# A two-layer attention and mixture-of-experts kernel: the first router's logits made with tokens on the partitions, and GpSimd's scatters of a batch issued in one go

## What is computed

```python
logits = jax.nn.relu(x @ rw1 + rb1) @ rw2 + rb2      # rw1 128x512, rw2 512x8
vals, ids = jax.lax.top_k(logits, K)                 # K = 2 of E = 8
probs = jax.nn.softmax(vals, axis=-1)
...
m = jax.nn.one_hot(ids_f, E, dtype=jnp.int32)
pos = jnp.cumsum(m, axis=0) - 1                      # place in the expert's queue
...
disp = jnp.zeros((E, CAP, Cx), x.dtype).at[ids_f, pos_c].add(xr * keep[:, None])
h = jax.nn.relu(jnp.einsum('enc,ech->enh', disp, ew1) + eb1[:, None, :])
eo = jnp.einsum('enh,ehc->enc', h, ew2) + eb2[:, None, :]
y = eo[ids_f, pos_c] * (probs_f * keep)[:, None]
```

## Time and profile before

| | |
|---|---|
| median of 3 runs | 906.22 us (905.99 to 906.40) |
| the profiled execution | 906.78 us, of which the span from the first to the last instruction is 905.0 us |
| granted TensorE clock over the span | 0.966 |
| PE busy | 772.4 us (85%) |
| DVE busy | 684.2 us (76%) |
| ACT busy | 629.4 us (70%) |
| POOL busy | 630.8 us (70%) |

### The profile page before, as it was taken

One profiled execution on the slowest core, in us unless ns is written; L12 is line 12 of the kernel. 1 busy time (PEld: TensorE's weight loads), 2 busy tenths in 40 slices (PEclk: granted clock), 3 DMA queues, 4 the chain that ended last, 5 costly groups with the idle time before them and its releaser, 6 DMA issues. The chain is left out here.

```text
span 905.0 us, 18379 instructions
## 1 busy us (share of the span) xinstructions
PE 772.4 (85%) x6152; PEld 468.8 (52%) x6152; DVE 684.2 (76%) x2029; ACT 629.4 (70%) x972; POOL 630.8 (70%) x416
## 2 busy tenths in 40 slices
PE   3978656678998799288889989999999999999997
PEld 1344212224443366132235757777777777777775
DVE  7859999975775587598999878666767666666654
ACT  3755333414445587168889988898989888889895
POOL 5008999810677546466998997686868686868695
PEclk9979898999999799689999999999999999999999
DMA  5899400018100120442600000000000000000000
GB/s 152 118 119 185 147 0 0 18 27 236 33 16 7 44 63 25 126 112 56 196 1 1 1 3 1 13 0 12 0 12 0 12 0 12 0 0 12 0 14 13
DMA packets 52794, 40.48 MB, mean 45 GB/s; under 512 B 6060, under 2 KB 44735, under 8 KB 52735
## 3 DMA queue, kind: packets, MB, share of 16 engines
q1 hardware_dynamic: 49662, 37.28, 18.7%
q0 software_dynamic: 3072, 2.51, 1.0%
HBM read 18.07 MB, written 14.88 MB: 36 GB/s over the span
## 5 line engine op out<-in xcount | busy, mean ns | idle before, releaser
L759 POOL TENSOR_TENSOR scratch<-scratch 128x1024 f16<-128x1024 f32 x128 | 272.8, 2134 | 84.6 <-ACT scratch L1216 82.4
L1877 DVE SCALAR_TENSOR_TENSOR resid<-PS,coef,resid 128x128 f32<-128x128 f32 x512 | 144.0, 344 | 108.7 <-PE PS L1929 103.2
L1929 PEld LDWEIGHTS PS<-A,scratch 128*128 128x128 f16 x3456 | 203.4, 98 | 37.8 <-POOL scratch L759 4.8
L1929 PE MATMUL PS<-A,scratch 128*128 128x128 f16 x3456 | 217.1, 219 | 3.9 <-POOL scratch L759 1.6
L1929 PE MATMUL PS<-A 128*128 (+1 forms) x768 | 186.8, 379 | 0.7 <-issue 0.2
L1212 ACT ACTIVATE scratch<-PS,cols 128x512 f32<-128x512 f32 x256 | 163.8, 683 | 25.8 <-PE PS L1929 18.9
L1216 ACT ACTIVATE scratch<-scratch 128x1024 f16<-128x1024 f32 x128 | 135.3, 1057 | 5.0
L1929 PE MATMUL PS<-scratch,ident 128*128 128x512 f32 x160 | 85.0, 651 | 41.1 <-DVE scratch L1392 41.0
L624 POOL TENSOR_TENSOR scratch<-A 128x1024 f32<-128x1024 f32 x32 | 75.7, 2393 | 59.1 <-DVE A L1363 56.7
L1929 PEld LDWEIGHTS PS<-A 128*128 128x128 f16 x768 | 70.7, 98 | 66.5 <-issue 0.7
L669 POOL DMA_INDIRECT disp<-A,scratch x64 | 62.9, 982 | 36.5 <-issue 30.1
(11 more groups left out here) (342 smaller groups left out, 1332.9 us busy)
## 6 DMA issues: line engine op xcount, KB each, us to landing
A<-A SPq DMA_DIRECT2D x22, 256.0 KB, 7.5
y_rows<-zeros SPq DMA_DIRECT2D x8, 512.0 KB, 6.0
A<-y_rows SPq DMA_DIRECT2D x14, 256.0 KB, 3.9
disp<-zeros SPq DMA_DIRECT2D x4, 528.0 KB, 21.3
resid<-in_L_attn_x SPq DMA_DIRECT2D x8, 256.0 KB, 3.8
A<-scratch SPq DMA_DIRECT2D x8, 256.0 KB, 7.2
A<-in_L_ffn_ew SPq DMA_DIRECT2D x1, 2048.0 KB, 12.7
A<-scratch SPq DMA_DIRECT2D x32, 64.0 KB, 2.0
```

The lines of the kernel that those rows point to most:

```text
L759: pool.tensor_tensor(h_low[n % 4], h_full[n % 2], h_high[n % 4], SUB).then_inc(S("m1_low"), 1)
L1877: last = STT(out=resid[:, g, :], in0=bank(4 + e % 2)[:, t * C:(t + 1) * C], scalar=coef[b % 2][:, t, e:e + 1], in1=resid[:, g, :], op0=MUL ...
L1929: return nc.tensor.matmul(o, l, r, start=start, stop=stop)
```

## The change

`router_logits_T` and the transposes go, and so does ScalarE's copy. `router_logits(b)` now holds a 128x128 tile of the hidden layer and streams the 128x8 weights: 4 tiles of tokens by 4 parts of the hidden layer, 16 f32 matmuls of 8 columns, straight into bank 5 with tokens on the partitions. It stands where `router_logits_T` stood, ahead of `transpose5(b+1)`. It waits for VectorE to have read the last batch's logits out of bank 5. `relu5` waits for `lg5_mm` instead of `lgT5_mm`. GpSimd's wait ahead of the fifth scatter goes. ScalarE waits for its own last `hid5` before it uses banks 0 to 3 for the weights.

```diff
                 for t in range(NT):
-                    if t == NT // 2 and b + 1 < B:
-                        pool.wait_ge(S("lg5_mm"), at(b + 1))
-                    elif t == NT // 2:
-                        pool.wait_ge(s_eb2_mm, 1)
                     for k in range(TOP0):
...
-                act.wait_ge(S("lgT5_mm"), at(b, 2))
+                act.wait_ge(S("lg5_mm"), at(b, 2))
...
-            def lgT5_copy(b):
-                act.wait_ge(S("lgT5_mm"), at(b))
-                act.wait_ge(S("lg5_mm"), at(b, 1))
-                A_(lg5_T, bank(5)[0:E0, :], ACT.Copy).then_inc(S("lg5_T"), 1)
...
-                lgT5_copy(b)
...
+            act.wait_ge(S("hid5"), at(B * HC0 - 1))
             for k in range(EARLY):
...
-                TT(lg5[u], bank(6)[:, 0:NT * E0].rearrange("p (n e) -> p n e", e=E0),
+                TT(lg5[u], bank(5)[:, 0:NT * E0].rearrange("p (n e) -> p n e", e=E0),
...
-            def router_logits_T(b):
+            def router_logits(b):
                 pe.wait_ge(S("hid5"), at(b * HC0 + HC0 - 1))
-                pe.wait_ge(S("lg5_T"), at(b, 1))
-                for h in range(HC0):
-                    last_mm = mm(bank(5)[0:E0, :], w_r2[:, h, :], hid[b % 2][:, h, :], start=h == 0, stop=h == HC0 - 1)
-                last_mm.then_inc(S("lgT5_mm"), 1)
-
-            def router_logits(b):
-                pe.wait_ge(S("lg5_T"), at(b))
-                pe.wait_ge(S("placed"), at(b, 1))
-                for t in range(NT):
-                    last_mm = nc.tensor.transpose(bank(6)[:, t * E0:(t + 1) * E0], tile(lg5_T, t), ident[0:E0, 0:E0])
+                pe.wait_ge(S("lg5_added"), at(b, 1))
+                for t in range(NT):
+                    for h in range(HC0):
+                        last_mm = mm(bank(5)[:, t * E0:(t + 1) * E0], tile(hid[b % 2][:, h, :], t), w_r2[:, h, :],
+                                     start=h == 0, stop=h == HC0 - 1)
                 last_mm.then_inc(S("lg5_mm"), 1)
...
-                router_logits_T(b)
+                router_logits(b)
                 if b + 1 < B:
                     transpose5(b + 1)
                 if b and b + 2 < B:
                     variance_o(b + 2)
-                router_logits(b)
                 if b == 0:
```

More of the change, by code:

```diff
@@ L128, in build @@
                     "r0_decay", "r_coef", "p2_copied", "o_sq", "o_std", "x_std",  "hid5",
-                    "rows5", "lg5_T", "m0_hid",  "m1_cT", "m1_hid", "m1_high",
+                    "rows5", "m0_hid",  "m1_cT", "m1_hid", "m1_high",
                     "xn7",  "kq_high", "v_copied7", "gk_copied", "sg_7", "gate_ln", "gate_high",
@@ L136, in build @@
                     "gate_low", "yg1_ready", "z_added",   "mlp_added", "xn12", "split_low", "m0_low", "xdT", "x_low", "lg12_added", "lg_less", "z_stats", "hid11_low"],
-            "pe": ["transposed", "proj_q", "proj_k", "proj_b", "proj_g", "proj_v", "ss_head", "r0_acc", "r_q", "r_acc", "p2_mm", "centred", "o_var", "proj_o",  "hid5_mm", "lgT5_mm", "lg5_mm", "counts", "trd",
+            "pe": ["transposed", "proj_q", "proj_k", "proj_b", "proj_g", "proj_v", "ss_head", "r0_acc", "r_q", "r_acc", "p2_mm", "centred", "o_var", "proj_o",  "hid5_mm", "lg5_mm", "counts", "trd",
                    "m0_hid_mm", "m0_out_mm", "m1_cT_mm", "m1_hid_mm", "m1_out_mm", "m1_bias_mm",  "kq_mm", "v_mm7", "g_mm7", "gk_mm", "r1_k", "r1_e",
@@ L380, in build @@
         id5 = [v.rearrange("p (k n) -> p k n", k=TOP0) for v in routing(192, 8)]
-        lg5_T = carve(8)[0:E0, 512:1024]
         place = by_expert(carve(8)[:, 0:32])
```

## The result

The changed kernel took **920.19 us** (median of 4 runs, 919.71 to 923.03), the kernel before 906.31 beside it (4 runs, 905.99 to 907.47): a ratio of 1.015, 95% interval 1.0138 to 1.0162. The forecast was 904.6 with a range up to 909.6. It became slower, by the way that the prediction held for the first of its rivals: TensorE's clock falls behind the new logits.

The account below looks back on a forecast made before the run. GpSimd's scatters were taken to decide stage 5's end, by 0.7 us over the barrier. Batch 0's 1.1 plus GpSimd's 0.55 gave 1.65 us: 906.22 - 1.65 = 904.6 us, own range 903.9 to 905.2, whole range 903.5 to 909.6.

Parts of the forecast that it names:

- the first of its rivals: Stage 5: TensorE's clock falls in the new logits and the kernel gets slower, 926 us (915 to 945); 16 in 100.
- TensorE's clock: Stage 5: 4.8 us of few columns per batch might lower the clock; the forecast took it as staying at 1.00.
- Against it: TensorE is never idle there: Argument against the clock falling in stage 5's new logits, a case given 16 in 100.
- So little streaming makes it fall: Stage 5: read from the clock's fall to 0.50 at 298, behind 4 us with twelve small matmuls.
- 3 more: Steady batches, if the clock falls and is back halfway: a batch costs 3 us more, 20 us over seven batches.
- The new logits: TensorE, stage 5: 32 instructions at 0.105 us each, 3.4 us, hidden in steady batches behind the wait for `normalise5`.
- Batch 0: Stage 5's first batch: routing starts 1.1 us earlier, and this gain is carried to batch 6.
- the 0.55: GpSimd, batch 6: without the middle wait its scatters start 0.55 us (0.44 to 0.66) sooner after their slots.
- the contention of scatters and VectorE might fall too: Stage 5: aside in the rival that GpSimd's whole 3.94 us wait comes back, 902.9 or better; 8 in 100.
- What is late next: End of stage 5: SP and stage 6 follow the scatters; the barrier strand, its slots 2.2 us earlier, stays in front.
- the barrier strand: Entry of stage 6: TensorE passes the barrier and runs unread matmuls, done 0.7 us before the scatters let stage 6 start.
- the rival of 0.125 an instruction: Stage 5: `transpose5` waits for slower new logits, 0.3 us in each of five batches, 906.6 us; 7 in 100.

Follow-up runs that it names:

- the run of the scatters alone: The kernel before with only GpSimd's wait in the middle of a batch's scatters left out: 907.44 us, ratio 1.0015.
- few columns: The kernel before with 14 unread f32 products of 128x8 added behind the old logits of each batch: 944.30 us, ratio 1.042.
- many columns: The kernel before with 15 unread f16 products of 128x512 added behind the old logits of each batch: 930.37 us, ratio 1.0266.

## Why the prediction was wrong

**The step that failed** is the choice in "TensorE's clock": "Whether loading keeps the clock up no row tells", and the sum then went by a clock of 1.00 with 16 in 100 on the other side. The runs show that it does not stay up in this stretch. Behind 28 or 32 loads of 128x128 with 8 columns each, it is at 0.50 in every batch, though the engine is busy; behind the same time with 512 columns a load it is not. "Against it: TensorE is never idle there" was the wrong argument. It is true, 69.9 of 70.0 us, and has no weight. "So little streaming makes it fall" turned out right, but its row did not show it: in the 4 us ahead of 298 TensorE was busy for only 0.76, so idleness would have explained that fall as well. All seven falls in the trace of the kernel before come behind 4 us in which TensorE was busy for 2.5 us or less.

**The size of that rival** was 20 us (926); it is 14. The pieces held: a fall lengthens the work from `variance_o` to the next logits by 8.80 - 5.91 = 2.9 us in the batch at 269.9, as its "3 more". But the step between routings grows by 1.94 us on the mean. In some batches the clock is back sooner: the step from 246.4 grew by only 1.6. And the loop is no longer the one through VectorE: before, TensorE idled 8.8 of 71 us, and this slack takes the first part of the longer work.

**The new logits** are 32 instructions in 231.60 - 227.92 = 3.68 us, 0.115 each, where 0.105 was taken and 0.101 to 0.125 were the bounds. At 1.00 they would still be hidden behind the 3.78 until `normalise5`, but with 0.1 to spare, not 0.3.

**Batch 0** won 0.4 and not 1.1. From the start of the logits to the routing it is 218.88 - 215.10 = 3.78, against 4.73 before: 0.95 of the 1.1 is there. But the logits start 0.55 later (215.10 for 214.55): stage 5 began 0.35 later, a difference from stages that the change does not touch, and the six matmuls ahead of the logits took 1.66 for 1.46. Nothing was carried on: the clock is down from 218.8.

**GpSimd.** That each batch starts 0.8 after its slots was right: 240.60 against slots at 239.8 (in batch 0 it is 0.96, 225.52 against 224.56). So was the 0.55, with 0.44 to 0.66 around it: in the run of the scatters alone batch 6 starts at 291.48, 0.78 after its slots and not 1.44. What was missed is that the place of the scatters against VectorE's work changes too. That "the contention of scatters and VectorE might fall too" was named, with the wrong sign: 1.3 us later in that run.

**What is late next.** The prediction would be wrong "if something other than the rows of `disp` releases stage 6". It does: in the changed kernel it is the barrier strand, not because it got much longer, but because GpSimd caught up. It hangs on the slots of batch 7, as was predicted: the routing is 13.2 late, TensorE is through the barrier 13.45 late (326.30 against 312.85), and the last scatter only 11.7. This is a consequence and adds 0.9 us (12.6 against 11.7).

**The chances.** Slower stood at 26 in 100, and the range stopped at 909.6 because the falling clock was left out of it whole. The trace had no stretch as thin as the new one, so no row spoke for a clock of 1.00 behind it either; 16 in 100 rested on the busy engine alone. Of the 26, 4 belong to no time: the rival of 0.125 an instruction stands for 906.6, which is "same".

**Small slips in the sums.** At 0.125 an instruction batch 0 wins 4.73 - 4.25 = 0.5 and not 0.6. The 902.9 is counted from the profiled 906.78; from the median it is 902.3. And 1.91 is the length of a row, to be held against `project0`'s length of 1.16, not against its 1.0 from start to start. None of these moves the forecast.

## What to carry to other kernels

Here a form of a product that loads 128x128 weights for 8 columns kept TensorE busy and still lost its clock, and the loss landed on the work behind it: 3.2 us a batch of such work cost 13.9 us more than 3.2 us of work with 512 columns. Before replacing few instructions of 512 columns by many of 8, add up the stretches with few columns in a row, the neighbours included, and look in the trace for what the granted clock did behind the nearest such stretch; that it was never idle is no argument. If the freed steps are off the loop, as here, there is little to win against that risk (1.65 us were forecast).

## What the runs showed of the hardware

- The granted clock falls to 0.50 with TensorE busy for 70.9 of 71 us (few columns: mean 0.85) and stays at 1.00 with 70.2 of 71 (many columns). It also stays at 1.00 through 6.5 us of f32 loads with 128 columns each, of which the loading takes 6.29.
- A scatter of GpSimd can hold a short VectorE instruction from SBUF to SBUF until it ends: the cast of 128x8 takes 171 to 173 ns when it starts 0.16 to 0.36 us behind the scatter's start, and 295 to 409 when it starts 0.56 to 0.67 behind. Moving GpSimd's issues against it cost 1.2 us over seven batches.
- The same kernel takes 906 to 907 us on some chips and 929 to 933 on others, where its granted clock is hardly lower (0.96 against 0.97), and with results of TensorE that reach ScalarE 3.5 to 4.35 us after their modelled end (the changed kernel there, waits labelled `remote`; the longest such wait is 7.3). On these the price of each part of the change is another one. The cause stays open.
